# A gated attention and feed-forward kernel: outputs added by accumulating DMAs, the first down quarter loaded in two parts, and late weight sums made later

## The reference

```python
def reference(x, Wq, bq, Wk, bk, Wv, bv, Wo, bo, SU_ug, SU_dp, Wscale_ug, Wscale_dp, W_up, W_gate, W_down):
    xn = layernorm(x)
    q, k, v = xn @ Wq.T + bq, xn @ Wk.T + bk, xn @ Wv.T + bv
    phi_q, phi_k = elu(q) + 1, elu(k) + 1
    context = phi_q * cumsum(phi_k * v, axis=1) * SCALE      # along the tokens of a chunk
    s = context @ Wo.T + bo
    h = fwht(xn * SU_ug)                                     # Hadamard transform over 512
    up, gate = h @ W_up.T * Wscale_ug[:2048], h @ W_gate.T * Wscale_ug[2048:]
    g = silu(fwht(silu(gate) * up * SU_dp) @ W_down.T * Wscale_dp)   # transform over 2048
    return x + s * g
```

## Time and profile before

| | us |
|---|---|
| three runs | 1305.65, 1305.70, 1307.26 |
| median | 1305.7 |
| profiled execution | 1306.03 |
| its span | 1304.2 |
| TensorE busy in the span | 1260.7 (97%), 5896 matmuls |
| VectorE busy | 952.3 (73%) |
| ScalarE busy | 617.4 (47%) |
| GpSimd busy | 76.0 (6%) |

### The profile page before, as it was taken

One profiled execution on the slowest core, in us unless ns is written; L12 is line 12 of the kernel. 1 busy time (PEld: TensorE's weight loads), 2 busy tenths in 40 slices (PEclk: granted clock), 3 DMA queues, 4 the chain that ended last, 5 costly groups with the idle time before them and its releaser, 6 DMA issues.

```text
span 1304.2 us, 16175 instructions
## 1 busy us (share of the span) xinstructions
PE 1260.7 (97%) x5896; PEld 570.9 (44%) x5896; DVE 952.3 (73%) x1440; ACT 617.4 (47%) x910; POOL 76.0 (6%) x121
## 2 busy tenths in 40 slices
PE   5998999989999999999999999999999999999997
PEld 3543444434444444444444444444444444444443
DVE  6989999877655778686884778776773777775714
ACT  5894565631235565552334555554234555554212
POOL 1001001111000000010012001000001000000000
PEclk9999999999999999999999999999999999999999
DMA  9533563677473366655367334323525443232431
GB/s 376 211 129 121 177 218 130 232 269 279 173 290 129 128 237 219 226 180 213 137 220 257 137 108 151 129 97 102 207 87 162 162 130 129 97 129 73 130 126 68
DMA packets 63759, 220.96 MB, mean 169 GB/s; under 512 B 7232, under 2 KB 17216, under 8 KB 48960
## 3 DMA queue, kind: packets, MB, share of 16 engines
q1 hardware_dynamic: 44576, 175.88, 37.4%
q0 software_dynamic: 9648, 30.94, 7.0%
q10 hardware_dynamic: 9456, 13.11, 3.0%
HBM read 166.40 MB, written 53.50 MB: 169 GB/s over the span
## 4 chain that ended last, share of the span: by engine, by line
PE 51%; DVE 7%; issue 3%; ACT 3%; ACTq 0%; DVEq 0%; POOL 0%
PE bank L2358 39%; PE bank L2424 7%; PE bank L2544 4%; PE bank L2449 2%; DVE work L1549 1%; DVE work L1548 1%; ACT work L1193 1%; DVE work L1630 1%; ACT work L1196 1%; DVE work L1614 1%; DVE ctx L1723 0%; DVE ctx_max L1481 0%; DVE ctx L1722 0%; DVE h_all L1991 0%; DVE work L1620 0%
## 5 line engine op out<-in xcount | busy, mean ns | idle before, releaser
L2358 PE MATMUL bank<-xops,ring 128*128 128x512 f16 x2772 | 602.7, 379 | 10.4 <-DVE work L1630 4.6
L2358 PEld LDWEIGHTS bank<-xops,ring 128*128 128x128 f16 x2772 | 269.5, 98 | 342.7 <-issue 10.5
L2238 PE MATMUL bank<-xops,ring 128*128 128x512 f16 x1008 | 225.1, 379 | 1.2 <-DVE ring L1786 1.2
L1176 ACT ACTIVATE work<-bank 128x512 f32<-128x512 f32 x198 | 117.8, 595 | 216.5 <-PE bank L2358 202.0
L1614 DVE TENSOR_TENSOR work<-bank,work 128x512 f32<-128x512 f32 x198 | 133.2, 685 | 114.0 <-PE bank L2358 101.5
L2544 PE MATMUL bank<-h_all,ring 128*128 128x512 f16 x768 | 168.4, 382 | 3.7 <-DMA ring<-scr_d 3.6
L2238 PEld LDWEIGHTS bank<-xops,ring 128*128 128x128 f16 x1008 | 97.9, 98 | 124.6 <-issue 8.9
L2544 PEld LDWEIGHTS bank<-h_all,ring 128*128 128x128 f16 x768 | 75.4, 98 | 96.1 <-DMA ring<-scr_d 4.1
L1223 ACT ACTIVATE h_all<-work 128x512 f16<-128x512 f32 x116 | 70.3, 624 | 61.4 <-DVE work L1657 56.8
L1666 DVE TENSOR_TENSOR h_all<-work,h_all 128x512 f16<-128x512 f32 x116 | 79.2, 685 | 10.9 <-ACT h_all L1223 9.6
L1620 DVE SCALAR_TENSOR_TENSOR work<-work 128x512 f32<-128x512 f32 x64 | 44.1, 689 | 49.2 <-ACT work L1196 48.7
(11 more groups left out here) (278 smaller groups left out, 1306.1 us busy)
## 6 DMA issues: line engine op xcount, KB each, us to landing
ring<-scr_g SPq DMA_DIRECT2D x72, 1024.0 KB, 4.8
ring<-scr_d SPq DMA_DIRECT2D x16, 1024.0 KB, 5.2
scr_g<-ring SPq DMA_DIRECT2D x22, 512.0 KB, 3.2
h_all<-in_ug_t SPq DMA_DIRECT2D x8, 1024.0 KB, 13.2
ring<-in_down_t SPq DMA_DIRECT2D x6, 1024.0 KB, 6.2
scr_g<-ring POOLq DMA_DIRECT2D x12, 512.0 KB, 4.2
work<-in_x_t SPq DMA_DIRECT2D x6, 1024.0 KB, 6.9
scr_g<-h_all POOLq DMA_DIRECT2D x12, 512.0 KB, 3.7
```

The lines of the kernel that those rows point to most:

```text
L1176: act.activation(tile(g, j), chain_bank(g)[:, :], ACT.Copy).then_inc(copied, 1)
L2238: mm = pe.matmul(plain_bank(g, j)[:, :], at[:, s, 2 * dh + kk, r, :], xops[:, kk, xs, PLAIN_B[dh][c], :], start=(n == 0), stop=(n == len(t ...
L2358: mm = pe.matmul(to[:, :], weight_of(slot, s, b, kk), at, start=(a == 0 and m in (P1, P2, P5)), stop=(a == 5), skip_group_check=True)
```

## The change

It has six parts.

1. The outputs of all pairs, but for the last three tiles of the last pair (LAST_BY_DVE), are added to x by accumulating DMAs of POOL. For pair 0 these stand on POOL's list behind store_sums of pieces 8 and 11, for pair 1 behind its stores of down units. The loads of x into result tiles go, except for three tiles at the end. SP's stores wait for the accumulations.
2. LATE_OUTS has only outputs 6 and 7 of pair 2, in groups 0 and 1. Outputs are made one by one between the O sums. In the last pair the last tile's partial sum times gate plus x is made ahead (last_ahead), with a gate scaled by ScalarE (scaled_gate), and two instructions follow the last product (last_output).
3. The first down quarter is loaded in two parts: blocks 0 to 2 (768 KB) at group 18, the last block (256 KB) when it is stored.
4. The late sums are made in groups 6 to 15 (pieces 12 to 21), 16 and 17 (O). The O blocks are loaded by POOL. The statistics steps (S_STATS, STATS_AT) are moved by one or two groups.
5. The first down block begins at tile 21 and not 20, and the third piece's butterflies are at tiles 25 and 26, not 24 and 25.
6. ScalarE's order at the end of a pair: O copies ahead of the next pair's x halves. VectorE's order at the end of pair 1 is changed likewise, and SP's stores of outputs 6 and 7 come after load 5, not 7.

```diff
-LATE_OUTS = {0: (4,), 1: (5,), 4: (6, 7)}
+LATE_OUTS = {0: (6,), 1: (7,)}
+OUTS_BEHIND = (8, 11)
+LAST_BY_DVE = 3
-DOWN_FROM, DOWN_EVERY = 20, 16
+DOWN_FROM = (21, 36, 52, 68)
-S_LATE_FROM, S_LATE_O = 4, {15: GROUPS, 17: GROUPS + 1}
-S_STATS = (20, GROUPS)
-STATS_AT, LATER_STATS_AT = (16, 18), (8, 10)
+S_LATE_FROM, S_LATE_O = 6, {16: GROUPS, 17: GROUPS + 1}
+S_STATS = (GROUPS - 1, GROUPS)
+STATS_AT, LATER_STATS_AT = (18, 20), (8, 10)
...
-        FLY_AT[8 * _i + 8], FLY_AT[8 * _i + 9] = ((_i, 0),), ((_i, 1),)
+        _n = 8 * _i + (9 if _i == 2 else 8)
+        FLY_AT[_n], FLY_AT[_n + 1] = ((_i, 0),), ((_i, 1),)
...
-def added_by_dma(p):
-    return SEVEN_FROM <= p < PAIRS - 1
+def added_by_dma(p, n):
+    return p < PAIRS - 1 or n < 2 * TB - LAST_BY_DVE
...
+            def load_first_tiles():
+                for e in range(KB - 1):
+                    sp.wait_ge(d_stored[e], 16)
+                src = scr_d[QUADS[0], :, 0:KB - 1, :].rearrange("p e n -> p (e n)")
+                sp.dma_start(ring[:, 3, 0:1024 * (KB - 1)], src).then_inc(slot_loaded[3], 16)
             def load_first_quad(n):
                 if n == 0:
-                    for e in range(KB):
-                        sp.wait_ge(d_stored[e], 16)
-                elif n >= 2:
+                    sp.wait_ge(slot_loaded[3], 16)
+                    sp.wait_ge(d_stored[KB - 1], 16)
+                    sp.dma_start(ring[:, 3, 1024 * (KB - 1):], scr_d[QUADS[0], :, KB - 1, :]).then_inc(slot_loaded[3], 16)
+                    return
+                if n >= 2:
...
             for n in range(PIECES):
                 if n + 1 < S_RING:
                     load_blocks(n + 1)
+                elif n + 1 in (GROUPS, GROUPS + 1):
+                    load_o_blocks(n + 1)
                 store_sums(n)
+                if n in OUTS_BEHIND:
+                    for t in range(TB):
+                        add_tokens(0, TB * OUTS_BEHIND.index(n) + t)
...
+                if p == PAIRS - 1:
+                    c, t = tile_at(p, 2 * TB - 1)
+                    act.wait_ge(gate_ready, 8 * p + 8)
+                    act.wait_ge(out_scaled, p + 1)
+                    act.activation(scaled_gate, gate_of(c, t), ACT.Copy, scale=o_out[:, 0:1]).then_inc(gate_scaled, 1)
                 o_groups(p)
             def o_groups(p):
                 g = GROUPS
-                copy_sum(p, g, 0)
+                for n in range(3):
+                    copy_sum(p, g, n)
+                copy_sum(p, g + 1, 0)
                 if p < SEVEN_FROM:
                     x_high(p + 1, 0)
-                copy_sum(p, g, 1)
-                copy_sum(p, g, 2)
-                copy_sum(p, g + 1, 0)
...
+            def last_ahead(p):
+                c, t = tile_at(p, 2 * TB - 1)
+                dve.wait_ge(copied, 3 * nth(p, GROUPS + 1) + 2)
+                dve.wait_ge(gate_ready, 8 * p + 8)
+                prep.after(dve.tensor_tensor(o_of(c, t), gate_of(c, t), o_of(c, t), ALU.mult))
+                dve.wait_ge(res_loaded, 16 * LAST_BY_DVE)
+                prep.after(dve.tensor_tensor(res_of(c, t), res_of(c, t), o_of(c, t), ALU.add))
+            def last_output(p):
+                c, t = tile_at(p, 2 * TB - 1)
+                dve.wait_ge(product_done, products_to(p, GROUPS + 1, P3))
+                dve.wait_ge(gate_scaled, 1)
+                prep.after(dve.tensor_tensor(o_of(c, t), left_bank(GROUPS + 1)[:, :], scaled_gate, ALU.mult))
+                dve.tensor_tensor(res_of(c, t), res_of(c, t), o_of(c, t), ALU.add).then_inc(out_ready, 1)
...
-                for j in (C11, C22, C12):
-                    add(p, GROUPS, j)
-                pair_outputs(p, (0, 1))
+                add(p, GROUPS, C11)
+                pair_outputs(p, (0,))
+                add(p, GROUPS, C22)
+                pair_outputs(p, (1, 2))
+                add(p, GROUPS, C12)
+                pair_outputs(p, (3,))
                 add(p, GROUPS + 1, C11)
+                pair_outputs(p, (4,))
+                if p == PAIRS - 1:
+                    last_ahead(p)
                 add(p, GROUPS + 1, C22)
-                pair_outputs(p, (2, 3))
-                add(p, GROUPS + 1, C12)
+                pair_outputs(p, (5,))
+                if p == PAIRS - 1:
+                    pair_outputs(p, (6,))
+                    last_output(p)
+                else:
+                    add(p, GROUPS + 1, C12)
```

More of the change, by code:

```diff
@@ L190, in down_of @@
 def down_of(n):
-    e, at = divmod(n - DOWN_FROM, DOWN_EVERY)
-    return (e, at) if 0 <= e < KB else (None, None)
+    for e, first in enumerate(DOWN_FROM):
+        if 0 <= n - first < 16:
+            return e, n - first
+    return None, None
 def late_sums(g):
@@ L225, in loads_into @@
     own = sum(dmas_of(*at) for at in ALL_LOADS[:to] if slot_of(*at) == slot_of(p, n))
-    return (4 if slot_of(p, n) in (3, 4) else 0) + own
+    return ({3: 5, 4: 4}.get(slot_of(p, n), 0)) + own
 def slot_held_by(p, n):
@@ L354, in gate_of @@
             return h_tile(t, c % 2)
+        scaled_gate = work[:, 0, :]
         def ct_sum(p, n):
@@ L765, in spread_stats, with load_last_res, store @@
                              scr_m.rearrange("t p -> (t p)").partition_broadcast(P)).then_inc(spread_loaded, 16)
[L767 to L779, removed]
-                    sp.dma_start(out[c, t * P:(t + 1) * P, :], x_res[:, t, :]).then_inc(out_stored[t], 16)
-            def load_pair_res(p):
-                for c in range(2):
-                    for t in range(TB):
-                        sp.dma_start(res_of(2 * p + c, t), x_t[2 * p + c, :, t, :]).then_inc(res_loaded[c], 16)
-            def store_pair(p, ns):
+            def load_last_res():
+                for n in range(2 * TB - LAST_BY_DVE, 2 * TB):
+                    c, t = tile_at(PAIRS - 1, n)
+                    sp.dma_start(res_of(c, t), x_t[c, :, t, :]).then_inc(res_loaded, 16)
+            def store(p, ns):
                 for n in ns:
-                    d, j = OUT_ORDER[n]
-                    c, t = 2 * p + CHUNK_OF[j], d + 2 * ROW_OF[j]
-                    if added_by_dma(p):
-                        sp.wait_ge(res_added[n % TB], 32 * (p - SEVEN_FROM) + 16 * (n // TB + 1))
+                    c, t = tile_at(p, n)
+                    if added_by_dma(p, n):
+                        sp.wait_ge(res_added[n % TB], 32 * p + 16 * (n // TB + 1))
                     else:
@@ L847, in _ @@
                     spread_stats(1)
-            store(0)
-            load_res(1)
+            store(0, range(TB))
             load_first_quad(2 * KB - 1)
@@ L855, in _ @@
                         if p <= SEVEN_FROM:
[L856 removed]
+                            store(p - 1, range(TB, 2 * TB))
                         else:
[L858 to L860 removed]
+                            store(p - 1, range(6))
+                    if p > SEVEN_FROM and n == 5:
+                        store(p - 1, (6, 7))
                     if n == GROUPS + (4 if p < SEVEN_FROM else 3) and p < PAIRS - 1:
@@ L865, in _ @@
                 if p < SEVEN_FROM:
-                    load_res(2 * p)
-                    store(2 * p)
-                    load_res(2 * p + 1)
-                elif not added_by_dma(p):
-                    load_pair_res(p)
-            store_pair(PAIRS - 1, range(8))
+                    store(p, range(TB))
+                elif p == PAIRS - 1:
+                    load_last_res()
+            store(PAIRS - 1, range(8))
             for t in range(TB):
@@ L940, in load_blocks, with load_o_blocks @@
                         .then_inc(s_loaded, 16)
+            def load_o_blocks(n):
+                pool.wait_ge(s_summed, n)
+                for k in range(KB):
+                    pool.dma_start(s_raw(n)[:, k, :, :], attn_rows(wo_t, n - GROUPS)[:, k, :, :]).then_inc(s_o_loaded, 16)
             def store_sums(n):
@@ L1355, in o_groups @@
                     load_unit(2)
-                copy_sum(p, g + 1, 2)
+                take(p, g + 1, C21)
                 if p < SEVEN_FROM:
@@ L1359, in o_groups @@
                     load_unit(3)
-                take(p, g + 1, C21)
             def silu_outs(c):
@@ L2528, in down_part @@
                     n = KB * cc + a
-                    slot, loads = 3 + n % 2, n // 2 + 1
+                    slot, loads = 3 + n % 2, n // 2 + 1 + (n % 2 == 0 and (n > 0 or ts[-1] == TB - 1))
                 else:
```

78 lines of the change are left out of this document (41 added, 37 removed).

## The result

The changed kernel took 1297.70 us (median of four runs, 1296.61 to 1299.55), the kernel before 1305.68 (four runs): ratio 0.9939, interval 0.9922 to 0.9956, so 8.0 us faster. The forecast was 1289.8 with a range of 1285 to 1296: the sign was right, half of the gain is missing, and the time lies 1.7 us above the range. The profiled execution of after took 1299.55, the longest of its four runs; its span is 1297.7, 6.5 less than before.

The account below looks back on a forecast made before the run. TensorE, busy 1260.7 of 1304.2 us, was taken as the bound, leaving its stalls, clock and tail. Gains 0.1 + 5.3 + 4.4 + 4.1 + 0.8 + 1.2 = 15.9; 1306.03 - 15.9 - 0.33 = 1289.8 us, range 1285.0 to 1296.0.

Parts of the forecast that it names:

- (a): First pair, down block one tile later: TensorE's 3.33 us of waits become about 3.2, a gain of 0.1.
- (b): First down quarter in two loads: TensorE's 3.58 us wait and 1.7 of low clock behind it go, gain 5.3.
- (c): Pair 1, late sums two groups later, O blocks by POOL: three stalls shrink or go, gain 4.4 us.
- none above 0.5 in groups 6 to 15: Sign of being right: no TensorE gap above 0.5 us in pair 1's groups that now make late sums.
- a load may now wait for its store: Pair 1: SP's piece load may wait for that piece's store, still some 20 us before TensorE needs it.
- with nothing else queued: Pair 1: on POOL the O blocks stand only behind the previous sum's store; 0.2 us taken off for late landing.
- Rival 3: Pair 1: late sums' stalls only move, as VectorE has the same work two groups later; 3.1 us lost, chance 0.12.
- (d): Tail behind TensorE's last matmul: VectorE ends 4.6 us sooner, less 0.5 for ScalarE's scaling, gain 4.1.
- a sign of being wrong that the prediction names: Tail: SP's last stores leaving well behind VectorE's end would show the forecast wrong.
- Rival 2: Tail is set by the accumulation of output 4, not by VectorE; 4.1 us lost, 1293.9, chance 0.12.
- (e): Smaller stalls: 0.8 us gained at 648.18 by ScalarE's new order, 1.2 in pair 3; other parts cost nothing.
- Rival 4: Stores waiting for accumulations delay pair 1's weight loads on SP; 1311.8 us at a 50 us landing, chance 0.03.

Follow-up runs that it names:

- experiment 4: Changed kernel with the first down quarter loaded as one 1 MB load again, once all four blocks are stored: 1301.28 us, ratio 0.9959.
- experiment 1: Changed kernel with late sums, O sums and statistics back in their old groups, O blocks still loaded by POOL: 1295.62 us, ratio 0.9916.
- experiment 9: Changed kernel with piece 23's sum in group 18, output 4 stored last but one, last gate scaled later, ScalarE's block loads issued sooner: 1290.00 us.
- experiment 5: Changed kernel with only POOL's statistics loads moved one piece later, behind the O blocks of piece 23: 1294.47 us, ratio 0.9907.
- experiment 3: Changed kernel with only the sum of piece 23 one group later, in group 18 in place of 17: 1293.09 us, ratio 0.9892.
- experiment 8: Changed kernel with the first down block at tile 20 and the third piece's butterflies at tiles 24 and 25 again: 1297.82 us, ratio 0.9941.

## Why the prediction was wrong, and where it was right

**(a)** Right. Three waits were forecast at 1.2, 0.5 and 1.5; the timeline of after has them:

```profile
106.87 1.13 PE L2334 MATMUL bank<-ring,hada 128*128 128x512 f32 x2 [1.09 <-DVE ring L1931]
...
114.83 2.76 PE L2289 MATMUL bank<-xops,ring 128*128 128x512 f16 x12 [0.37 <-DVE ring L1809]
...
125.79 1.12 PE L2334 MATMUL bank<-ring,hada 128*128 128x512 f32 x2 [1.30 <-DVE xops L1955]
```

1.09, 0.37 and 1.30, in all 2.8 where 3.2 was reckoned, and undoing the shift changed nothing that can be measured. That VectorE's list fixes the end of the level, whichever tile TensorE is at, was the right way to see it.

**(b)** Right in the mechanism; the size holds for the two profiled executions. TensorE does not stand, the granted clock is 1.00, and 23 matmuls fit where 15 did:

```profile
288.00:292.60 4.60, 4.60 (x23) 2.08 (x22) 4.60 (x9) 0.00 (x0) 1.86 (x4) 1.00 0.71 237
```

Up to pair 1 5.74 us were gained, where (a) and (b) together had 5.4. That they agree so well is in part luck: 3.58 us of wait and the low clock behind it are what one execution of before had. With one load again, experiment 4 had 2.12 and no low clock there, and lost 2.0. The Trainium skill's fixed cost of each transfer ("DMA: Bandwidth & Descriptors", section "Anatomy of one DMA — SWDGE (gpsimd) path"; the page fits it to DMAs of GpSimd, and SP issues these loads), which speaks against two loads, did not decide: TensorE waited for neither, and in experiment 4 for the one of 1 MB.

**(c)** Wrong, and this is the step that failed: "gains of 1.6 and 1.5" and "for which I take 0.2 off". The gains came (0.20 and 0.32 are left where 1.79 and 1.77 stood, and nothing of the 1.53). But the sign "none above 0.5 in groups 6 to 15" failed, with 0.99. What I missed is that every late sum needs blocks that are loaded one group ahead. I had even written that "a load may now wait for its store", and costed it by TensorE's lead alone: not late, hence free. Its cost lay elsewhere, in whom that load now meets, as I read the times: ScalarE's load. Its median landing rose from 3.2 to 4.1 us, and VectorE waited 4.1 us in six places in place of 0.7 in two. That the new places of the sums cost this is shown by experiment 1, and that it passes through VectorE's waits for the blocks by experiment 9; that the one load slows the other was not tested by itself. And the O blocks, for which I took 0.2, cost 3.44 and 1.6 us of low clock: "with nothing else queued" was false, as the moved statistics loads stand ahead of them on POOL. Experiment 5 moves only these loads and shows it. Rival 3 had the place right and the cause wrong: it blamed VectorE's own work, and it was VectorE's waits.

**(d)** The mechanism was right and the size was not. VectorE's part shrank by 4.3 us, and ScalarE's scaling cost 0.46 where 0.5 was taken. The term that was mis-sized is the accumulation of output 4: "at 5.1 the store of output 4 leaves at 1296.3, ahead of the last output". Issued at 1287.46, it held SP's stores 4 to 7 until 1293.2, so that they left one behind the other, the last at 1294.55, 1.27 after VectorE's end (a sign of being wrong that the prediction names); and that one took 2.7 to land where 2.0 was reckoned. In full, 4.3 - 0.5 - 1.3 - 0.7 = 1.8, against 1.68 measured. What the sum left out are the three stores behind that of output 4: they left 0.4 to 0.5 us apart, 1.3 in all, so even from 1296.3 on the last one would have left behind VectorE's end at 1297.1. Experiment 3 shows it: the accumulation landed in 4.9, and the last store was 0.47 behind. Rival 2 was thus half true. The six other profiles with this tail gained 2.3 to 2.7 of the 4.1.

**(e)** Right: 0.99 for 0.8 and 1.19 for 1.2. Not forecast is a loss of 0.54 at the start of pair 2, where TensorE waits 0.38 for a weight load, beside which the accumulations of pair 1's last outputs run; a kernel without these was not tried. Each run with the change has this wait, of 0.3 to 0.7 us, and of 2.0 in experiment 4, so "All cost nothing" was not quite so. Rival 4 did not come: no weight load of pair 1 was late.

Experiment 9 is the fastest version: 1290.0, 7.7 us below the changed kernel and 16.3 below the one before beside it. That this is near the 1289.8 forecast for the change as it stood proves nothing for the forecast: it gets there with four edits more.

## What to carry to other kernels

When a producer is moved later, the loads of its product get a new time of issue, and what they then run beside has to be costed, not only whether they are late themselves. What counts is the lead of a load, from its issue to its first use, against its landing while another load runs. On a queue, list by name what stands ahead of the one transfer with the least slack, and of the steps that the same change moves there. At the end of a kernel, the stores behind one that waits in an ordered queue leave one after the other when it is released, and have to be counted; putting it last but one made the last store leave at once, though the time showed little of it here.

## What the runs showed of the hardware

TensorE's clock did not fall behind each wait, and the length of the wait did not decide it. It fell behind 3.58 us in before (0.63 granted), 3.44 in after (0.61) and 2.00 in experiment 4 (0.62), and not behind 3.31 in experiment 8, nor behind 2.66 and 2.12 in experiment 4. The window behind the wait of experiment 8:

```profile
564.40:568.70 4.30, 4.21 (x20) 1.98 (x21) 4.14 (x7) 3.81 (x7) 0.00 (x0) 1.00 0.01 6
```

Two waits of about the same length, at the same place of the program, thus differ by 1.6 us of clock. This, and the length of single loads, may be why the changed kernel's runs spread over 2.9 us while those of experiment 9, which has no wait above 1.3 us but the long one at the start, lie within 0.65; the spread itself was not tested. The accumulating DMAs of after, 29 of 256 KB, landed in 3.6 to 9.7 us, median 5.9.
